# Upper parts of keys and queries: copied by GpSimd in place of ScalarE

## The reference

```
c_q  = x @ W_DQ ;  c_kv = x @ W_DKV                      # latents, 32 wide
Q = [c_q @ W_UQ , rope(c_q @ W_QR)]                       # 16 heads, 8 + 4
K = [c_kv @ W_UK , rope(x @ W_KR)] ;  V = c_kv @ W_UV
w = softmax(causal(clip(Q K^T, -80, 80)) / sqrt(12))
x = layernorm(x + (w V) @ W_O)
e = argmax(x @ gate_w^T + gate_b + expert_bias)           # one of 8 experts
x = layernorm(x + relu(x @ w1[e] + b1[e]) @ w2[e] + b2[e])
```

## Time and profile before

| | |
|---|---|
| three runs | 469.29, 470.72, 471.51 us, median 470.72 |
| the profiled execution, its own time | 466.76 us |
| its span, first to last instruction | 465.0 us |
| TensorE matmul busy | 427.2 us (92%) |
| VectorE busy | 365.1 us (79%) |
| ScalarE busy | 363.5 us (78%) |
| GpSimd busy | 130.9 us (28%) |

### The profile page before, as it was taken

The page is one execution under the profiler, slowest core; times in us unless marked ns, Lnnn a source line. Parts: engine busy times, 40 slices in busy tenths (PEclk is TensorE's granted clock), DMA queues, the critical chain, the costliest instruction groups (busy, mean ns, idle before and its releaser), DMA issues. The chain is left out here.

```text
span 465.0 us, 12398 instructions
## 1 busy us (share of the span) xinstructions
PE 427.2 (92%) x4259; PEld 230.8 (50%) x4259; DVE 365.1 (79%) x838; ACT 363.5 (78%) x580; POOL 130.9 (28%) x133
## 2 busy tenths in 40 slices
PE   7899999999999999999999999998899998599980
PEld 5543433444344434433443444343344797599980
DVE  4488779889896988899869889898978688467670
ACT  1598998999889999898899999889889565366650
POOL 7000000015005001311310015014001576878883
PEclk9899999999999999999999999999999999899995
DMA  3756646863462263063307603461420257567710
GB/s 106 171 142 138 141 125 137 184 189 88 95 139 70 64 168 67 13 149 81 92 12 160 137 2 87 93 144 48 139 48 2 76 147 192 143 186 217 196 54 5
DMA packets 33181, 51.67 MB, mean 111 GB/s; under 512 B 5675, under 2 KB 16337, under 8 KB 33120
## 3 DMA queue, kind: packets, MB, share of 16 engines
q1 hardware_dynamic: 25504, 37.04, 33.8%
q10 hardware_dynamic: 5344, 9.57, 7.6%
q0 software_dynamic: 2272, 4.27, 2.7%
HBM read 20.82 MB, written 5.33 MB: 56 GB/s over the span
## 5 line engine op out<-in xcount | busy, mean ns | idle before, releaser
L935 ACT ACTIVATE prob<-ring 128x1024 f32<-128x1024 f32 x288 | 277.3, 1037 | 32.5 <-PE ring L1095 30.8
L1113 PE MATMUL o_acc<-prob,v_stat 128*32 128x512 f32 (+3 forms) x1536 | 153.7, 495 | 8.2 <-ACT o_sb L965 5.6
L1095 PE MATMUL ring<-queries,keys 32*128 32x512 f32 (+3 forms) x1536 | 121.0, 380 | 0.9 <-ACT prob L935 0.9
L1095 PEld LDWEIGHTS ring<-queries,keys 32*128 32x128 f32 x1536 | 65.2, 183 | 72.4 <-issue 36.1
L597 DVE TENSOR_SCALAR prob<-prob 128x2048 f32<-128x2048 f32 x64 | 77.3, 1220 | 9.2 <-ACT prob L935 9.1
L611 DVE SCALAR_TENSOR_TENSOR prob<-prob,mask_hi 128x1024 f32<-128x1024 f32 (+1 forms) x80 | 80.3, 1003 | 0.0
L508 POOL TENSOR_TENSOR rstd<-var_eps,const 128x4 f32<-128x4 f32 x8 | 14.5, 1812 | 227.8 <-DVE var_eps L654 227.8
L610 DVE TENSOR_SCALAR prob<-prob 128x1024 f32<-128x1024 f32 (+1 forms) x80 | 64.3, 804 | 16.6 <-ACT prob L935 16.5
L1022 ACT ACTIVATE prob<-ring,b1T 128x128 f32<-128x128 f32 x156 | 44.7, 369 | 31.2 <-PE ring L1213 26.6
L517 POOL DMA_INDIRECT by_expert<-xrow,index x32 | 43.9, 1371 | 79.4 <-DVE index L706 71.7
L1113 PEld LDWEIGHTS o_acc<-prob,v_stat 128*32 128x32 f32 x1536 | 34.3, 108 | 56.4 <-issue 35.1
(11 more groups left out here) (106 smaller groups left out, 311.6 us busy)
## 6 DMA issues: line engine op xcount, KB each, us to landing
queries<-parts SPq DMA_DIRECT2D x62, 256.0 KB, 3.8
v_stat<-in_w ACTq DMA_DIRECT2D x34, 256.0 KB
keys<-parts SPq DMA_DIRECT2D x64, 128.0 KB, 2.4
queries<-by_expert SPq DMA_DIRECT2D x39, 66.0 KB, 2.7
xrow<-in_x_rows SPq DMA_DIRECT2D x8, 264.0 KB, 4.4
xT<-in_x_T SPq DMA_DIRECT2D x8, 256.0 KB, 4.2
v_stat<-in_w SPq DMA_DIRECT2D x5, 256.0 KB
out<-prob,queries POOLq DMA_INDIRECT x39, 3.2
```

The lines of the kernel that those rows point to most:

```text
L935: act.activation(prob[u % P_SLOTS][:, 2 * half:2 * half + 2, :].rearrange("p h s -> p (h s)"), slot(u, half)[:], ACT.Exp, scale=SCALE).the ...
L1095: last = pe.matmul(out[:, j % 2 * QC + off:j % 2 * QC + off + w], keys[hg][r, kt * P:(kt + 1) * P], queries[hg][r, qc, part, QC - w:QC], s ...
L1113: last = pe.matmul(o_acc[j * VW:(j + 1) * VW, QC - w:QC], v_stat[b % 2][:, hg, kt, j, :], prob[u % P_SLOTS][:, j, off:off + w], start=begi ...
```

## The change

`upper_of` leaves ScalarE's program and enters GpSimd's, as a `tensor_copy` with the same waits and the same increment. On ScalarE it stood one step after the project, between two exponentials; on GpSimd it stands in the project's own step, ahead of that step's routing DMA or power. VectorE's two instructions (L579, L587) stay where they are. Before step 0 the copies stand after GpSimd's tables.

```
# gpsimd, added
+            def upper_of(b, hg, c):
+                i = PROJECT_NO[b, hg, c]
+                pool.wait_ge(proj_out, i + 1)
+                if i >= 2:
+                    b0, hg0, c0 = PROJECTS[i - 2]
+                    pool.wait_ge(kq_in[hg0][c0], (b0 + 1) * 64)
+                pool.tensor_copy(parts[i % 2][:, 0, :], whole_kq[i % 2][:]).then_inc(upper_part, 1)
...
+            for first_job in FIRST_JOBS:
+                if first_job[0] == "project":
+                    upper_of(0, *first_job[1:])
             for u in range(B * UB):
+                if step_job(u, "project"):
+                    upper_of(*step_job(u, "project")[1:])
                 if route_at(u):
                     route(*route_at(u))
# scalar, removed
-                act.activation(parts[i % 2][:, 0, :], whole_kq[i % 2][:], ACT.Copy).then_inc(upper_part, 1)
...
             for first_job in FIRST_JOBS:
-                if first_job[0] == "project":
-                    upper_of(0, *first_job[1:])
...
             for u in range(B * UB):
                 exp(u, 0)
-                if step_job(u - 1, "project"):
-                    upper_of(*step_job(u - 1, "project")[1:])
                 exp(u, 1)
```

## The result

The changed kernel takes 467.42 us (median of 6 runs, 465.51 to 468.31) where the kernel before takes 470.88 on the same chip (6 runs, 469.29 to 471.51). The ratio is 0.9931, 95% interval 0.9907 to 0.9954: faster by 0.7%, some 3.4 us, where 474.6 was forecast.

A forecast was written before the change was run, and what follows sets the result against it. TensorE, busy 92%, was taken as the bound, so only its waits come back. Terms summed to +3.8 us on 466.76, giving 470.6, scaled by 1.0082 to 474.6 us; 8-in-10 range 466.5 to 480.

The forecast's parts named there:

- s: VectorE's price where it has no gap: GpSimd's copy plus 0.05 us of handing over, 0.75 us (0.59 to 0.95).
- the first rival: Faster: the copy passes beside masked clip L611, only the handing over is exposed; -4.1 us, 466.6 us, chance 0.20.
- (a): Steps 0 to 5, batches 1 to 3: a 0.39 us gap goes, two copies are exposed; +1.11 us.
- (b): Steps 7 to 11, batches 1 to 3: step 7's 0.44 us is lost again, step 8's copy nearly fits; +0.1 us.
- (d): Steps 23 to 25: copies hidden at plain clips, 0.44 us won and kept.
- (c): Steps 18 to 23, batches 0 to 2: gap shrinks 0.52 us, first copy 0.16 short, second exposed; +0.39 us.
- (e): Batch 0: +0.55 us in steps 1 and 2, -0.44 in step 7, then (c) and (d); together +0.06 us.
- (f): Before step 0: copies start after GpSimd's tables, moving L587 from 12.30 to 12.55; +0.25 us.
- a copy group well above its least duration: Sign of being right: 32 copies on GpSimd whose mean is well over their least duration.
- the `o_sb` waits near zero: Sign of being right: TensorE's waits at L1113, 14 times and 5.6 us before, go to near zero.
- The wait of the lower parts for GpSimd: Sign of being right: a new wait of VectorE's lower part for GpSimd of 5 to 9 us.
- the wait at the flip: Sign of being right: TensorE's wait at the flip of step 5 grows from 0.34 to above 1.5 us.

The follow-up runs named there:

- the rest alone: Changed kernel, but the three projects before step 0 are copied by ScalarE, all later ones by GpSimd; 468.93 us, 0.9959 of the kernel before.
- The start alone: Kernel before, but the three projects before step 0 are copied by GpSimd, all later ones by ScalarE; 469.91 us, 0.9979 of the kernel before.
- the moved DMAs: Kernel before, but ScalarE's two DMA issues for the first queries stand behind the second upper part; 469.16 us, 0.998 of the kernel before.

## Why the prediction was wrong, step by step

**The step that failed is the price of an exposed copy, s = 0.75 us.** It stood on two choices. The copy's own time was set midway between the fill and the select of the earlier trace rows, 0.70; it is 0.61, inside the bounds, nearer to the fill, whose slope was the better guide for an instruction with one input. The larger error was "the copy has VectorE's port to itself or waits": it was put to wait for the plain clip and then to stop VectorE for all of its length. The wait is right (0.47 us after the clip in the places shown). But VectorE pays neither for the copy's whole length nor for a hand-over, and not in a wait of L587: the masked clip becomes 0.41 us longer, by the part of the copy that goes with its columns (0.61 less 0.19 for a copy of one column). With s = 0.41 for 0.75, steps 0 to 5 become -0.39 + 0.82 = +0.43; s lies just under the 0.47 from which the first rival said it decides.

**(a), predicted +1.11 per batch, measured +0.03 on TensorE and +0.04 on VectorE's chain.** Of the miss of 1.07, s makes 2 x 0.34 = 0.68, and 0.33 is a term that had no place in the sum: GpSimd's queue has another order, and the two clips that were longer beside routing DMAs are so no more. The row for it was in view (1.15 us at 194.20 in the earlier trace rows) and was used only as evidence on the port. The last 0.08 is the overlap of rows: a gap of 0.39 that closes frees 0.47.

**(b), +0.1, measured 0.0; (d), -0.44, measured -0.45.** Right in mechanism and size. The 0.42 won in step 7 is lost by step 12, and the 0.45 won in step 25 is kept.

**(c), +0.39, measured -0.10.** The terms hold but s: at 0.41 the first copy fits into the 0.59 that is left of the gap, and -0.52 + 0.41 = -0.11.

**(e), batch 0, +0.06, measured -1.07.** At s = 0.41 its first term, +0.55, would be +0.21; it is -0.25. The sum charged TensorE with VectorE's chain, as in (a), but here TensorE doesn't wait for it: VectorE's clip of step 2 comes 0.14 us later after its whole_kq than before, and TensorE doesn't show it. What it shows is ScalarE's freed time: the weighing that came 1.08 us after its scores (28.38, 29.46) comes 0.83 after them (27.07, 27.90), and 0.83 too with the one-column copy on ScalarE (29.59, 30.42). The other terms are -0.28 for step 7, where -0.44 was put, and (c) and (d).

Terms (a) to (e) were to sum to +3.6 us, and by the steps they are -1.07 + 2 x (-0.5), with about 0 in batch 3: -2.1. With s alone set right, at 0.41, the same sum gives about -0.5: that turns the forecast loss into no difference, and the gain that was measured is made by the terms that were missed. The experiments bear out both halves: with the reading taken out, a full batch gains 1.6 us, so the copies' hold on VectorE costs 1.1 of them; the one-column copy on ScalarE gains 1.2 to 1.4 without GpSimd, which shows the gain as ScalarE's freed time; and the rest alone is 0.4% faster.

**(f), the start, +0.25, measured -1.3 and -2.5.** The row of the second copy wasn't followed to what held it. The lower part was put at 12.55 and came at 12.19 (before: 12.30); the step assumed that ScalarE's DMA issues "only wait longer", and missed that the second copy had been queued behind them. The second lower part is 0.11 us earlier though the first whole_kq was 0.45 later in this execution (8.46 against 8.01). The larger part comes after it, where TensorE ran at 1.2 GHz for 3.4 us and now doesn't: its first scores start at 17.11 in place of 18.41. The start alone, and the moved DMAs, made the same gain. What in the start makes the clock fall isn't shown. In the time it is worth little, though: 0.998, with an interval that just holds 1.

**What was given back** was in no term: 1.3 us at the clock's fall near 323, at the wait of 2.47 us. Moving the plan takes away the wait and the fall, and wins 0.5% on the change. The fall is not the change's own: of the 12 profiles whose kernels have this wait 7 have a fall there, among them the one-column copy on ScalarE and the moved DMAs, and 5 have none, among them both of before.

**Smaller slips in the working.** The sentence with "3.9" means the sum that is given as 3.8. In rival 1, (c) is -0.47 and not -0.43. The power of 1.06 us, called alone, ran beside short instructions of VectorE (0.28 to 0.33 us). Nothing else hangs on these.

Of the marks that were named: no upper part on ScalarE, a copy group well above its least duration (1221 against 609 ns), and the `o_sb` waits near zero came true. The wait of the lower parts for GpSimd (2.5 us, all before step 0, not 5 to 9) and the wait at the flip (0.67, not above 1.5) didn't, and these two are the ones that hang on s.

**Open.** In the expert phase, first pair of profiles, the changed kernel's lead shrinks from 2.1 us to nothing and becomes a lag of 1.3; in the second pair it stays between 2.9 and 3.7. The first trace of after has waits of VectorE of up to 5.1 us there whose releaser the profile calls remote, and a half-clock stretch from 370.7; both traces of before and the second of after have no such wait. Here it is in the first of after and in the kernel with the moved DMAs, which has no copy on GpSimd:

```profile
367.23 0.29 DVE L893 TENSOR_TENSOR ys<-ring,x_b 128x128 f32<-128x128 f32 x1 [5.02 <-remote]
```
```profile
369.72 0.29 DVE L878 TENSOR_TENSOR ys<-ring,x_b 128x128 f32<-128x128 f32 x1 [5.11 <-remote]
```
The four profiles that were taken on one chip (both kernels once more, and the two copies of one column) don't have this wait, and the eight of the other experiments, all from another chip, have it, with either kernel as their base; the timed runs of the kernel before go the same way, with a median of 467.4 us on the first of these chips and 470.5 to 470.7 on the second. So this loss near 370 goes with where or when a profile was taken and doesn't need the change; what makes it isn't known. Nor is why the clock falls at the wait of 2.47 us in one kernel and not at that of 2.46 in the other.

## What to carry to other kernels

A copy moved to GpSimd isn't free while VectorE works from SBUF, but it costs VectorE less than its own length. Where it is issued beside a plain clip and an instruction with two SBUF inputs follows without a gap, charge VectorE the copy's time less that of a copy of one column (here 0.61 - 0.19 = 0.42 us, and only this size was run). Where VectorE has gaps, or only plain clips that were issued first, charge nothing. Where GpSimd is first, plain clips pay too, as the subtractions on GpSimd showed. When the sum is a difference of small terms, find each wait's true releaser in the engine's own order, DMA issues included, and look at what else changes place in the queue of the engine that receives the work. Where a trace has stretches at half clock, look for TensorE's waits ahead of them or under them, and take each price from the steps: here 1.3 us was given back at one. And profile both kernels on one chip before a difference between two traces is read.

## What the runs showed of the hardware

- GpSimd's copy of 128x512, fp32 to fp32r: 0.61 us alone; behind a clip that began first, plain or masked, it ends 0.47 us after it; it doesn't lengthen a plain clip that began first. A copy of one column: 0.19 us alone, 0.58 to 1.11 beside clips.
- The order decides who pays: with GpSimd's subtraction first (1.28 us), a clip of 1.22 us took 2.22; with the clip first, GpSimd's copy waits and the clip keeps its time.
- A fill only writes: it waits for the plain clip like the copy, and leaves the masked clip at 1217 ns, where the copy makes it 1287 on average and 1.62 us at most in the stretch shown.
- A wait of TensorE of 2.45 to 2.47 us, the same in 12 profiles, came with a granted clock of 0.50 for 3.4 us in 7 of them, which began from 0.5 us before the wait's end to 1.3 us after it, and with none in the 5 others. Such a stretch cost 1.3 us.
- Two DMA issues in ScalarE's queue took 1.41 us, and the copy behind them started 0.9 us after its data was ready.
